# A two-layer decoder on one core: a shared expert's output products moved between stages, and semaphore clearing moved into the next block

## The reference, cut to what matters

```python
D_HIDDEN, NUM_SHARED, NUM_ROUTED, TOP_K = 352, 2, 32, 6
def _expert_apply(xf, w1, b1, w2, b2):
    return jnp.maximum(xf @ w1 + b1, 0.0) @ w2 + b2
shared_out = (expert(sw1[0], ...) + expert(sw1[1], ...)) / NUM_SHARED   # over all tokens
logits = flat @ router_w + router_b
topk_p, topk_i = jax.lax.top_k(softmax(logits), TOP_K)
gates[token, topk_i] = topk_p / sum(topk_p)
routed_out = sum over e of gates[:, e] * _expert_apply(flat, rw1[e], rb1[e], rw2[e], rb2[e])
return shared_out + routed_out
```

## Time and profile before

| what | value |
|---|---|
| three runs | 3011.28, 3012.39, 3021.95 us; median 3012.39 |
| the profiled execution | 3017.26 us |
| its span, first to last instruction | 3015.5 us |
| busy, of the span | PE 90%, PEld 66%, DVE 49%, ACT 43%, POOL 37% |
| mean granted TensorE clock | 0.941 of full speed |
| routing of the second layer | from 2369.9 us |
| its expert blocks | from 2462.0 us |
| its sum, the last stage | from 2938.8 to 3014.3 us |

### The profile page before, as it was taken

The page is one execution under the profiler, slowest core; times in us unless marked ns, Lnnn a source line. Parts: engine busy times, 40 slices in busy tenths (PEclk is TensorE's granted clock), DMA queues, the critical chain, the costliest instruction groups (busy, mean ns, idle before and its releaser), DMA issues. The chain is left out here.

```text
span 3015.5 us, 47592 instructions
## 1 busy us (share of the span) xinstructions
PE 2722.7 (90%) x15710; PEld 1999.3 (66%) x15710; DVE 1482.6 (49%) x2654; ACT 1297.0 (43%) x2923; POOL 1127.5 (37%) x1031
## 2 busy tenths in 40 slices
PE   7888899996699498889999989999998879999987
PEld 5654443433588375568888879999997647777762
DVE  5576436776211427688875337677664431111115
ACT  2463425554111136466653248888872202222220
POOL 2352225665111205335554545555551211111116
PEclk9889999998699799989999999999999879999998
DMA  2342534210499414156667764444431139999987
GB/s 95 77 93 101 158 88 94 64 33 20 173 323 321 131 43 102 26 201 236 236 244 222 227 203 174 174 179 182 182 131 63 49 101 346 341 335 340 345 256 214
DMA packets 318224, 521.87 MB, mean 173 GB/s; under 512 B 35570, under 2 KB 168562, under 8 KB 309908
## 3 DMA queue, kind: packets, MB, share of 16 engines
q1 hardware_dynamic: 290132, 450.00, 46.1%
q0 software_dynamic: 13280, 43.53, 4.6%
q10 hardware_dynamic: 14688, 26.75, 2.5%
HBM read 365.39 MB, written 129.50 MB: 164 GB/s over the span
## 5 line engine op out<-in xcount | busy, mean ns | idle before, releaser
L1878 PE MATMUL ps<-moe_blocks_xgt,moe_blocks_w 128*128 128x128 f32 (+1 forms) x3000 | 357.1, 278 | 8.0 <-DMA moe_blocks_b1s<-rb_cols 5.2
L1878 PEld LDWEIGHTS ps<-moe_blocks_xgt,moe_blocks_w 128*128 128x128 f32 (+1 forms) x3000 | 343.6, 185 | 14.2 <-issue 12.5
L2843 POOL TENSOR_TENSOR normed<-normed,xa_core_rinv 128x257 f32<-128x257 f32 (+1 forms) x256 | 260.3, 1039 | 213.9 <-DVE xa_core_rinv L2767 213.9
L1949 DVE COPY moe_blocks_y<-ps 128x512 f32<-128x512 f32 x102 | 70.6, 692 | 452.4 <-PE ps L1860 452.4
L1860 PE MATMUL ps<-moe_blocks_w,moe_blocks_ht 128*128 128x512 f32 (+1 forms) x612 | 279.4, 593 | 0.0
L644 POOL TENSOR_TENSOR sa_w<-sa_w,sa_core_rinv 128x256 f32<-128x256 f32 (+3 forms) x128 | 159.2, 1253 | 226.8 <-DVE sa_core_rinv L591 226.8
L1825 POOL COPY moe_blocks_idx<-moe_index 128x1 uint32 (+1 forms) x102 | 18.7, 183 | 528.5 <-PE ps L1851 429.5
L2823 ACT ACTIVATE normed<-normed,xa_core_nmax,xa_rq 128x257 f32<-128x257 f32 (+1 forms) x256 | 206.7, 809 | 4.2
L2442 POOL TENSOR_TENSOR normed<-normed 128x512 f32<-128x512 f32 x96 | 150.6, 1569 | 116.1 <-DVE normed L2395 116.1
L1899 ACT ACTIVATE moe_blocks_xgt<-ps 128x512 f32<-128x512 f32 x102 | 60.9, 597 | 301.1 <-PE ps L1851 301.1
L881 DVE TENSOR_REDUCE xa_nmax<-ps 128x1 f32<-128x1024 f32 x128 | 149.2, 1217 | 58.4 <-PE ps L872 58.4
(11 more groups left out here) (359 smaller groups left out, 6627.5 us busy)
## 6 DMA issues: line engine op xcount, KB each, us to landing
moe_blocks_w<-L_ffn_rw SPq DMA_DIRECT2D x79, 704.0 KB
moe_blocks_w<-L_ffn_rw SPq DMA_DIRECT2D x79, 512.0 KB
k_parts<-xa_parts SPq DMA_DIRECT2D x64, 512.0 KB
v_parts<-xa_v_parts SPq DMA_DIRECT2D x128, 256.0 KB, 2.8
xa_parts<-k_parts SPq DMA_DIRECT2D x32, 1024.0 KB
xa_core_v<-v_parts SPq DMA_DIRECT2D x32, 1024.0 KB
moe_blocks_w<-L_ffn_w SPq DMA_DIRECT2D x23, 1408.0 KB
moe_y<-moe_blocks_y ACTq DMA_DIRECT2D x102, 256.0 KB
```

The lines of the kernel that those rows point to most:

```text
L1878: mm = nc.tensor.matmul(g.ps[0:fn, 2 + s % 2 + 2 * half, f * P:(f + 1) * P], w1s[s][:, k, half * F + f0:half * F + f0 + fn], xgt[:, s % 2, ...
L2843: ins = nc.gpsimd.tensor_tensor(prob[:, n % PR, lo:hi], prob[:, n % PR, lo:hi], rinv[:, n % PR, m:m + 1].to_broadcast([P, hi - lo]), ALU.mult)
```

## The change

First, leaving a stage only notes its semaphores; GpSimd clears them when the next block is opened, in its own list ahead of what it has in that block, and the second barrier is gone. One clear and one barrier stay at the end of the program. Second, the routing stage keeps the first shared expert's hidden values, turned gates, second weights and bias table (`keep`) in buffers of the outer stage; its `outputs` and additions are gone, and the gate transposes stand ahead of the second pick's index product. Third, in the last stage PE first makes `first(0)` to `first(3)`, which accumulate the first shared expert in banks 4 to 7, then the second's hidden chunks, then `last(0)` to `last(3)`, which accumulate the second's into the same banks, then `first(t)` and `last(t)` for tiles 4 to 7. The bias table holds both shared experts' rows, so that the bias product of the last stage and the load of its row are gone. The additions of the last stage, eight in all, then add both experts.

```diff
     def __exit__(self, *exc):
         if exc[0] is None:
-            self.nc.clear_and_free_semaphores(self.sems)
-            self.nc.all_engine_barrier()
+            Stage.retired.extend(self.sems)
         return self.stack.__exit__(*exc)
+
+def clear_retired(nc):
+    if Stage.retired:
+        nc.clear_and_free_semaphores(Stage.retired)
+        Stage.retired = []
+
+def open_block(nc):
+    clear_retired(nc)
+    return nc.Block()
...
-    with nc.Block() as block:
+    with open_block(nc) as block:
...
+    def keep(self, st):
+        self.w2, self.b2 = st.sbuf("sw2", [P, len(FCH), D]), st.sbuf("b2", [self.experts + NSH, D])
+        self.gt, self.ht = st.sbuf("gt", [self.experts + NSH, T]), st.sbuf("ht", [P, len(FCH), T])
+        self.w2_loaded = st.sem("w2_loaded")
...
-        sp.dma_start(self.b2[self.experts:self.experts + 1, :], a["L1_ffn_sb2"][e:e + 1, :]).then_inc(self.w2_loaded, 16)
+        sp.dma_start(self.b2[self.experts:self.experts + NSH, :], a["L1_ffn_sb2"]).then_inc(self.w2_loaded, 16)
...
+            def turn_gates():
+                pe.wait_ge(gated, 2 * top_k - 1)
+                for t in range(NT):
+                    mm = nc.tensor.transpose(g.ps[0:E, 3 - 2 * (t // HALF), t % HALF * P:(t % HALF + 1) * P], gates[:, t, :],
+                                             g.ident[:, :])
+                mm.then_inc(gates_turned, 1)
...
-            if r.shared:
-                pe.wait_ge(gated, 2 * top_k - 1)
-                for t in range(NT):
...
-                for t in range(HALF):
-                    outputs(t)
             for k in range(top_k):
                 pe.wait_ge(spots_done, k + 1)
                 pe.wait_ge(tokens_done, k + 1)
+                if r.shared and k == 1:
+                    turn_gates()
...
-            if r.shared:
-                for t in range(HALF, NT):
-                    outputs(t)
...
-            if r.shared:
-                dve.wait_ge(tables, 3)
-                for t in range(NT):
-                    dve.wait_ge(y_made, t + 1)
-                    nc.vector.scalar_tensor_tensor(g.x[:, t, :], g.ps[:, 4 + t % 4, :], share[:, 0:1], g.x[:, t, :],
-                                                   ALU.mult, ALU.add).then_inc(y_added, 1)
...
+            def first(t):
+                if t >= 4:
+                    pe.wait_ge(y_added, t - 3)
+                nc.tensor.matmul(g.ps[:, 4 + t % 4, :], kept.gt[:, t * P:(t + 1) * P], kept.b2[:, :], start=True, stop=False)
+                for f, (f0, fn) in enumerate(FCH):
+                    nc.tensor.matmul(g.ps[:, 4 + t % 4, :], kept.ht[0:fn, f, t * P:(t + 1) * P], kept.w2[0:fn, f, :],
+                                     start=False, stop=False)
+
+            def last(t):
+                pe.wait_ge(h_done, NF * (t // HALF + 1))
+                for f, (f0, fn) in enumerate(FCH):
+                    mm = nc.tensor.matmul(g.ps[:, 4 + t % 4, :], ht[0:fn, f, t * P:(t + 1) * P], w2[0:fn, f, :],
+                                          start=False, stop=(f == NF - 1))
+                mm.then_inc(y_made, 1)
+
+            pe.wait_ge(kept.w2_loaded, 64)
+            for t in range(HALF):
+                first(t)
             pe.wait_ge(w1_loaded, 32)
             for u in range(HU):
...
-            pe.wait_ge(w2_loaded, 48)
-            for t in range(NT):
...
-                nc.tensor.matmul(g.ps[:, 4 + t % 4, :], g.ones[0:1, :], b2[:, :], start=True, stop=False)
...
+            pe.wait_ge(w2_loaded, 32)
+            for t in range(HALF):
+                last(t)
+            for t in range(HALF, NT):
+                first(t)
+                last(t)
...
+        clear_retired(nc)
+        nc.all_engine_barrier()
```

More of the change, by code:

```diff
@@ L1458, in across @@
         return x.rearrange("p (o n) -> p o n", o=1).to_broadcast([P, NT, n])
-    with nc.Block() as blk:
+    with open_block(nc) as blk:
         if r.shared:
@@ L1697, in shared_expert, with _ @@
-        if pool_work is not None:
-            @block.gpsimd
-            def _(pool):
-                pool_work(pool, picks_added)
+            sp.dma_start(w2[0:FCH[2][1], 2, :], a["L1_ffn_sw2"][LAST, 256:F, :]).then_inc(w2_loaded, 16)
+            for t in range(NT):
+                sp.wait_ge(y_added, t + 1)
+                sp.dma_start(out[t * P:(t + 1) * P, :], g.x[:, t, :]).then_inc(stored, 16)
+            sp.wait_ge(stored, 16 * NT)
+        @block.gpsimd
+        def _(pool):
+            pool_work(pool, picks_added)
@@ L1746, in _ @@
             dve.wait_ge(share_set, 1)
-            if add_picks is None:
-                for t in range(NT):
-                    add(t)
-            else:
-                for t in range(HALF):
-                    add_picks(dve, t, picks_added)
-                for t in range(HALF):
-                    add(t)
-                    add_picks(dve, HALF + t, picks_added)
-                for t in range(HALF, NT):
-                    add(t)
+            for t in range(HALF):
+                add_picks(dve, t, picks_added)
+            for t in range(HALF):
+                add(t)
+                add_picks(dve, HALF + t, picks_added)
+            for t in range(HALF, NT):
+                add(t)
 def blocks_bound(experts, top_k):
@@ L2039, in moe @@
 def moe(nc, g, m, w1, w2, b1_cols, gated, out=None):
+    if m.shared:
+        m.loads.keep(m.stage)
     with Stage(nc, m.name + "_route") as ro:
@@ L2050, in beside_shared @@
         def beside_shared(gather, add_picks):
-            shared_expert(nc, g, su, m.a, 1, m.share, share_set, gather, m.top_k, add_picks, out)
+            shared_experts(nc, g, su, m.a, m.loads, m.share, share_set, gather, m.top_k, add_picks, out)
         combine(nc, g, su, m.top_k, m.places, m.best, m.y_dram, beside_shared if m.shared else None)
```

74 lines of the change are left out of this document (18 added, 56 removed).

## The result

| | median us | runs | lowest to highest |
|---|---|---|---|
| kernel before | 3016.39 | 4 | 3011.28 to 3021.95 |
| changed kernel | 2976.60 | 4 | 2972.98 to 2984.73 |

The ratio of changed to before is 0.9871, with a 95% interval of 0.9842 to 0.9901: 1.3% faster, where 1.2% was forecast. A second timing of the same changed kernel, beside the last group of experiments, gave 2975.91 us and 0.985 (0.9832 to 0.9868). The profiled executions took 3017.26 and 2977.32 us.

A forecast was written before the change was run, and what follows sets the result against it. Routing was taken as bound by DVE's chain, then PE alone; the last stage by gathers and DVE. Routing 24.8 plus clearing 14.5 minus last stage 4 gave 35.3 us off 3012.39: 2977 us, range 2965 to 2996.

The forecast's parts named there:

- Routing, tail: End of the second layer's routing block: without four output tiles and eight additions it ends after `block_row`, 20.4 us sooner.
- Routing, middle: Index picks in the routing block: 5.6 us hole on PE goes, new 1.2 us stall comes, so 4.4 us gained.
- rule on idle gaps: Routing block: skill's advice against longer gaps between matmul bursts, since the clock falls; priced at the 1.2 us stall.
- Clearing: Block boundaries: all line 68 barriers but one go, 15.9 us less what POOL gives back, taken as 14.5 us (10 to 16).
- Last stage: Last block: PE takes on the moved products and becomes the bound, about 4 us longer (2 to 8).
- Rival, last stage hides the work: Last block: PE's waiting absorbs the moved products, so the stage does not grow; 2973 us, chance 0.10.
- second rival: Boundaries: barriers covered something late anyway, so removing them gives nothing; 2991.6 us, chance 0.09.
- rule on fetches behind taken branches: Boundaries: skill says engines wait for code not held near; barriers may have covered this, leading to 2991.6 us.
- rival of a stage that grows by 12 us: Last block: every PE wait on DVE feeds back into later tiles, growth 12 instead of 4 us; 2985 us, chance 0.09.
- upper bound of 8 us: Last block: growth of 8 us, with the low clock level kept twice as long and a gather's slip.

The follow-up runs named there:

- gates early: Changed kernel with the gate transposes moved back behind the ranking products, into PSUM banks 6 and 7: 2977.22 us, ratio 0.9877 to the kernel before.
- the gap filled: Changed kernel with twelve more unused products (24 matmuls) in PE's hole ahead of the first index product: 2977.63 us, ratio 0.9847 to the kernel before.
- Move alone: Changed kernel with clear and second barrier at every stage's end again, only the output products moved: 2994.25 us, ratio 0.9931 to the kernel before.
- the clearing alone: Kernel before with only the deferred clears and the second barriers removed, output products unmoved: 3001.88 us, ratio 0.9956 to the kernel before.
- the one with the long low level: Changed kernel with no clears ahead of the blocks that POOL's gathers open: 2978.58 us, ratio 0.9872 to the kernel before.

## Why the prediction was right

The sign, the places and most of the terms were right. That the time comes out within 0.5 us (2977.1 worked out, 2976.6 measured) is partly luck. The forecast was 35.3 us less than a median of 3012.39; with a fourth run the median of before is 3016.39, and the change is 39.8 us, or 40.7 in the spans. The forecast change was 4.5 to 5.4 us too small, and the base lay 4.0 us low. Of the 5.4 us in the spans, the routing has 1.8, the last stage 1.5, the boundaries with the first layer's sum 0.2, and 1.9 lie in blocks from which nothing can be read. Term by term:

- *Routing, tail*: 20.4 us forecast, 20.2 measured: the release follows `block_row` by 0.38 us and not by 0.2, and it had stood 20.55 us behind. This was right.
- *Routing, middle*: the forecast had a new stall of 1.2 us on DVE ahead of the fourth pick, from transposes and products at the low level; it was 0.81. Right in place and cause: with the transposes taken out of the chain (gates early) it was nil, though the index products still took 1.93 us. The lengths came out as worked out, 1.89 and 1.93 us, but I had laid them end to end, where the product starts 1.54 us behind the transposes' start (2403.58 to 2405.12). The Trainium skill's rule on idle gaps ("TensorE: Matmul & The Clock Gate", section "Why this matters for your kernels") had been weighed there; the trace agrees with the fall of the clock. But the forecast charged the stall to the gap, and with the gap filled the level fell all the same and the stall stayed at 0.81 us, so no run shows a price of the gap by itself.
- *Routing, not foreseen*: 1.5 us more came from the logits at the stage's start, whose low clock level fell differently. It wasn't in the sum. Move alone, with the same routing program, doesn't have it; the clearing alone, with the routing of before, does.
- *Clearing*: 14.5 us forecast. The traces give 15.3 at the boundaries, less 0.6 at the first layer's sum; the run of the half alone gives 13.3 by medians. The size was right, its composition was not: the forecast took POOL's clears as 0.3 us a boundary. There were 71 clears instead of 37, and in the last block they delay the gathers by 1.0 us. In the changed kernel's profiled execution that is hidden, since PE is the bound; where the gathers end last, as in the changed kernel's second one, it need not be.
- *Last stage*: +4 us forecast, +2.5 measured. That PE would become the bound, start right behind the release, and keep DVE waiting at the first output tile's addition, with the fifth tile's picks behind it (3.26 us against 3 worked out), and at the last addition (1.27 us) all stands in this trace; over the seven executions of this block it was the bound in five. The size was off by two terms of half a microsecond: PE needed 74.7 us of the 75.3 worked out, and the release follows the last addition's end by 2.4 us where it had been 2.9; the last addition now stands 1.3 us apart from the three ahead of it, so their stores are further on their way, but no run separates this.
- *Rival, last stage hides the work*: falls, with the second rival, that boundaries give nothing: both halves run alone give, by medians, what the sum gave them (13.3 for 14.5 us, 20.9 for 24.8 - 4 = 20.8), and the last addition waits for PE. The Trainium skill's rule on fetches behind taken branches ("Runtime: NRT & Kernel Launch", section "Instruction fetch mechanics") would have led there; nothing in these runs shows such a wait. The rival of a stage that grows by 12 us didn't happen; its price was near once, +6.3 us, from the low level kept for 14 us and not from the waits on DVE that this rival spoke of. The upper bound of 8 us was there for this.

The products that were moved cost the last stage little though they are 30.6 us of PE's time: PE there was idle for 8.81 us at its start and in holes of 3.4 and 3.3 us later, its eight bias products went (8 of 1.05 us), and the gathers had set the end, with DVE's last addition done 2.4 us behind PE's last product. In the routing the second four of them cost 20.2 us, since behind `block_row` PE was the only one still needed, and the first four, made while DVE worked, 4.8 us.

## What to carry to other kernels

Work that an engine does alone at a stage's end is worth moving into a stage in which that engine waits for transfers, even if it then becomes the bound by a little; how much it costs there is the distance between its own sum of work and the other limit, and the second limit tells how much more is to be had (here 0.6 to 1.7 us for 8.4 us less). A barrier behind a barrier cost 0.33 us and the clear ahead of it some 0.2 more: nothing at one boundary, but 0.5% of this kernel over thirty. Put clears on an engine's list where it doesn't head the next chain, and count them in the trace, for their number can rise when they are collected.

## What the runs showed that I had not expected

- Deferring the clears took 71 range clears in place of 37, and a block's opening with six of them took POOL 1.0 us longer to its first gather. With none ahead of the gathers there were 48, in the kernel with the unmoved products.
- POOL's addition of 128x512 stopped a 0.19 us operation of DVE for 1.1 us, and an operation of 0.82 us too.
- Ten microseconds of filling matmuls in PE's hole kept the high level only until 2402.2, one product of small matmuls behind the filling.
- Programs with the same last block had it end by PE in five executions and by gathers and picks in two, with lengths of 76.9 to 78.2 us, and 81.8 in the one with the long low level.
- The low level at the start of the last block lasted between 4.4 and 14.3 us behind its release in executions of programs with the same matmuls there, PE being busy from 0.16 us on. What decides it is left open.
